# Graph attention on one core: rows gathered in plain edge order, each step a pair of an aligned group of 512 edges and a node tile

## The reference, cut to what matters

```
h = (x @ W).reshape(n, heads, ch)
e = alpha_src[src] + alpha_dst[dst];  e = where(e > 0, e, 0.2 * e)
m = segment_max(e, dst);  ex = exp(e - m[dst]);  s = segment_sum(ex, dst)
msg = h[src] * (ex / (s[dst] + 1e-16))[:, :, None]
out = segment_sum(msg, dst) + b
```

## Time and profile before

| | us |
|---|---|
| median of 3 runs (8891.62 to 8900.51) | 8892.6 |
| span of the profiled execution, first to last instruction | 8886.9 |
| median less span (what lies around it) | 5.7 |

### The profile page before, as it was taken

One profiled execution on the slowest core, in us unless ns is written; L12 is line 12 of the kernel. 1 busy time (PEld: TensorE's weight loads), 2 busy tenths in 40 slices (PEclk: granted clock), 3 DMA queues, 4 the chain that ended last, 5 costly groups with the idle time before them and its releaser, 6 DMA issues.

```text
span 8886.9 us, 230055 instructions
## 1 busy us (share of the span) xinstructions
PE 6173.7 (69%) x49885; PEld 5210.5 (59%) x50563; DVE 6168.8 (69%) x25428; ACT 4847.6 (55%) x11854; POOL 6191.5 (70%) x7562
## 2 busy tenths in 40 slices
PE   2466666666599999984666666666646666666665
PEld 2365656556588888873555555545445555656564
DVE  7799833333267676757999999999856666666665
ACT  4133333333245555534777777777647777777775
POOL 0377777777777777735777777777647777777775
PEclk9988888888899999986888888888755555555555
DMA  4233222222232323312222222222421111111114
GB/s 141 52 63 63 62 63 62 63 62 62 61 90 85 86 85 86 85 35 56 55 55 55 55 55 55 56 55 56 47 25 29 29 29 29 29 29 29 29 29 28
DMA packets 990923, 493.64 MB, mean 56 GB/s; under 512 B 830674, under 2 KB 841604, under 8 KB 990276
## 3 DMA queue, kind: packets, MB, share of 16 engines
q0 software_dynamic: 168832, 302.29, 15.6%
q1 hardware_dynamic: 701892, 169.48, 10.2%
q10 hardware_dynamic: 119840, 18.68, 1.3%
HBM read 356.53 MB, written 151.48 MB: 57 GB/s over the span
## 4 chain that ended last, share of the span: by engine, by line
issue 26%; POOL 21%; PE 20%; DVE 15%; DMA 7%; ACT 7%; DVEq 3%; ACTq 1%; POOLq 0%; SPq 0%; another core or an unknown queue 0%
POOL z_s L639 13%; POOL arena L689 8%; DMA arena<-table,arena 6%; PE ps_all L961 5%; PE ps_all L971 5%; ACT arena L825 3%; PE ps_all L984 3%; PE ps_all L981 2%; DVE arena L1494 2%; PE ps_all L1069 1%; ACT arena L857 1%; DVE arena L1580 1%; PE ps_all L993 1%; DVEq L385 1%; DVE ps_all L1232 1%
## 5 line engine op out<-in xcount | busy, mean ns | idle before, releaser
L689 POOL DMA_INDIRECT arena<-table,arena x3616 | 3527.3, 975 | 1421.4 <-issue 963.9
L639 POOL DMA_INDIRECT z_s<-arena x1660 | 1591.9, 959 | 850.8 <-issue 479.6
L1093 PE MATMUL ps_all<-arena 128*128 128x132 f32 (+1 forms) x7232 | 1584.7, 388 | 1.8 <-DVE acc L1597 1.8
L1093 PEld LDWEIGHTS ps_all<-arena 128*128 128x128 f32 x7232 | 1405.9, 288 | 2.7 <-issue 2.6
L1069 PE MATMUL ps_all<-ident_b,arena 128*128 128x128 bf16 x3616 | 465.3, 270 | 1311.8 <-DMA arena<-table,arena 1191.7
L825 ACT ACTIVATE arena<-lanes_b,arena 128x128 bf16<-128x128 bf16 x3616 | 1144.9, 386 | 349.1 <-DVE arena L1467 342.2
L1069 PEld LDWEIGHTS ps_all<-ident_b,arena 128*128 128x128 bf16 x3616 | 282.3, 117 | 1478.6 <-issue 844.4
L1494 DVE TENSOR_REDUCE arena<-ps_all 128x2 f32<-128x1024 f32 x904 | 1098.5, 1215 | 39.0 <-PE ps_all L1110 37.6
L849 ACT ACTIVATE arena<-ps_all 28x512 bf16<-28x512 bf16 (+1 forms) x904 | 527.5, 584 | 956.8 <-PE ps_all L1069 955.8
L744 ACT ACTIVATE arena<-ps_all 18x512 f32<-18x512 f32 x415 | 243.3, 586 | 1211.9 <-PE ps_all L948 1180.1
L1110 PE MATMUL ps_all<-arena,pick 128*128 128x512 bf16 x1809 | 694.6, 489 | 54.6 <-DVE arena L1494 24.3
(11 more groups left out here) (259 smaller groups left out, 15032.7 us busy)
## 6 DMA issues: line engine op xcount, KB each, us to landing
arena<-z_s SPq DMA_DIRECT2D x452, 264.0 KB, 2.7
arena<-table,arena POOLq DMA_INDIRECT x3616
arena<-rec_d SPq DMA_DIRECT2D x1660, 10.0 KB
z_s<-arena POOLq DMA_INDIRECT x1660
rec_d<-in_rec ACTq DMA_DIRECT2D x1, 16160.0 KB, 59.0
arena<-ids_d SPq DMA_DIRECT2D x904, 4.0 KB
arena<-pos_d SPq DMA_DIRECT2D x830, 0.5 KB
arena<-pos_d ACTq DMA_DIRECT2D x830, 0.5 KB
```

The costliest lines, as they stand in the source:

```text
L639: pool.indirect_dma_start(z_s, bass.IndirectOffsetOnAxis(ap=slot[:, g.slot(SLOTS), u:u + 1], axis=0), z_out[:, g.slot(SLOTS), u, :], None) ...
L689: pool.indirect_dma_start(g_rows[:, r, u * step + CODE_WORDS:(u + 1) * step], None, tables[n], bass.IndirectOffsetOnAxis(ap=ids[:, r, 0, u ...
L1093: mm = pe.matmul(ps[6][:, 0:out_w], a_hot_f[:, g.slot(4), u, :], g_msg[:, g.slot(4), u * out_w:(u + 1) * out_w], start=(u == 0), stop=(u = ...
```

## The change

The rows are no longer gathered group by group of the tiles, but in plain edge order: QUADS = 403 aligned groups of 512 edges cover all edges. One step ("visit") takes one pair of such an aligned group and a node tile that has edges in it. An aligned group that a tile boundary crosses is visited twice, so there are VISITS = 403 + 49 - 1 = 451 steps.

- SP and POOL run over the 403 aligned groups (`quad_pipeline`, peel 16, body 16); PE, ACT and DVE run over the 451 visits, with peel 16 and body 8 as before.
- `g_rows` becomes a ring of 16 aligned groups. SP loads only source numbers, and for group q waits for the messages of the last visit of group q - 16, read from a new table `done_by`.
- POOL waits for the landing of the previous aligned group before the last of its four gathers, and then counts it in `quads_in`.
- DVE finds the aligned group of a visit by register arithmetic (`quad_of`: visit number less tile number), and from it the ring slot for `logits` and `messages`, and the place of the destination numbers. These lie in SBUF for the whole layer (`node_of`), brought once by a DMA of 51,584 runs of 16 bytes that ACT issues at the start of the edge MLP.
- The codes no longer stand beside the gathered row but in a tile of their own (`coded`). A new DVE operation, `share_parts`, copies the three bf16 parts from the ring into it, after waiting for `quads_in`; PE transposes `coded` (32 columns) once that copy is done.

```diff
+QUADS = LINEAR // GE
+VISITS = QUADS + NT - 1
+RING = 16
+def quad_pipeline(eng, step, layer, each_round=None):
+    pipelined(eng, QUADS, 0, step, layer * QUADS, peel=RING, unroll=RING, each_round=each_round)
...
-                        sp.wait_ge(S("a_lane_ready"), g.back(SLOTS).done())
+                        sp.wait_ge(S(f"quads_in{n}"), Group(g.i, g.off - SLOTS, 0).done())
                         sp.sem_inc(S("sp_go"), 1)
-                        sp.wait_ge(S("neg_lane_ready"), g.back(SLOTS).done())
+                    if g.back(RING).exists():
+                        sp.wait_ge(S("msg_ready"), (freed.of(g.back(RING)) & COUNT_MASK) + n * VISITS)
...
-                    if g.back(SLOTS).exists():
-                        pool.wait_ge(S("msg_ready"), g.back(SLOTS).done())
-                        pool.wait_ge(S("turned"), g.back(SLOTS).done())
...
                     for u in range(U):
+                        if u == U - 1 and g.back(1).exists():
+                            landed(g.back(1))
...
+                def landed(g):
+                    pool.wait_ge(S(f"gathered_{g.slot(LANDING)}"), g.uses(LANDING, 16 * U))
+                    pool.sem_inc(S(f"quads_in{n}"), 1)
...
+            act.dma_start(node_of.rearrange("p (q u) -> p q u", u=U), ids_d[1:2, 0:LINEAR].rearrange("a (q p u) -> p (a q) u", p=P, u=U)
+                          ).then_inc(S("nodes_in"), 16)
...
-                        pe.wait_ge(S(f"gathered_{r}"), g.uses(SLOTS, 16 * U))
+                        pe.wait_ge(S("parts_ready"), g.done())
...
+                def quad_of(g):
+                    return (g.at - buckets.of(g)).with_bounds(min_val=0, max_val=QUADS - 1)
+                def gathered_rows(g):
+                    at = ((quad_of(g) & (RING - 1)) * slot_words).with_bounds(min_val=0, max_val=(RING - 1) * slot_words)
+                    return g_rows[:, bass.ds(at, U * row)]
...
-                    dve.tensor_tensor(lane, node, first, ALU.subtract).then_inc(S("a_lane_ready"), 2)
-                    dve.tensor_tensor(minus, first, node, ALU.subtract).then_inc(S("neg_lane_ready"), 2)
+                    for k, v in enumerate(visits):
+                        dve.tensor_tensor(lane[:, k, :], node_of[:, bass.ds(quad_of(v) * U, U)],
+                                          first_node[:, bass.ds(v.at, 1)].broadcast_to([P, U]), ALU.subtract).then_inc(S("a_lane_ready"), 1)
+                    dve.tensor_scalar(minus, lane, -1.0, None, ALU.mult).then_inc(S("neg_lane_ready"), m)
...
+                def share_parts(g):
+                    if g.back(SLOTS).exists():
+                        dve.wait_ge(S("turned"), g.back(SLOTS).done())
+                    parts = gathered_rows(g).bitcast(BF16).rearrange("p (u w) -> p u w", u=U)
+                    dve.wait_ge(S(f"quads_in{n}"), (quad_of(g) & COUNT_MASK) + 1)
+                    dve.sem_inc(S("dve_go"), 1)
+                    dve.tensor_copy(coded[:, r, :, CODE:CODE + 3 * heads], parts[:, :, 0:3 * heads]).then_inc(S("parts_ready"), 1)
...
                     for part in (shifts, codes, shifts):
                         next(part, None)
+                    share_parts(of(0))
```

More of the change, by code:

```diff
@@ L150, in attention_pipeline @@
 def attention_pipeline(eng, depth, step, layer, each_round=None):
-    pipelined(eng, GROUPS, depth, step, layer * GROUPS, peel=2 * SLOTS, unroll=SLOTS, each_round=each_round)
+    pipelined(eng, VISITS, depth, step, layer * VISITS, peel=2 * SLOTS, unroll=SLOTS, each_round=each_round)
+def quad_pipeline(eng, step, layer, each_round=None):
+    pipelined(eng, QUADS, 0, step, layer * QUADS, peel=RING, unroll=RING, each_round=each_round)
 class Chain:
@@ L240, in gnn_kernel @@
         group_tables = sb("group_tables", [64, ROW_GROUPS], I32)
-        bucket_of, first_edge = group_tables[0:1, :], group_tables[32:33, :]
+        bucket_of, done_by = group_tables[0:1, :], group_tables[32:33, :]
         src_tables = sb("src_tables", [64, ROW_GROUPS], I32)
@@ L263, in gnn_kernel @@
         tile_end = sb("tile_end", [NB, 3])
-        gap_wide = [sb(f"gap_wide{k}", [NB, P]) for k in range(2)]
+        tile_quad = sb("tile_quad", [NB, 1])
+        gap_wide = sb("gap_wide", [NB, P])
         here_lane = sb("here_lane", [P, 2])
@@ L673, in _ @@
                 pool.wait_ge(S("table_out"), 16 * (n + 1))
-                step = CODE_WORDS + row
                 def gather_rows(of):
@@ L1455, in edge_codes @@
                         return
+                    visits = [g] if h is None else [g, h]
+                    last, m = visits[-1], len(visits)
                     r, q = g.slot(SLOTS), g.slot(4)
-                    codes = g_rows[:, r:r + 2, 0:U * step].bitcast(BF16).rearrange("p k (u w) -> p k u w", u=U)
-                    lane, minus = lane_int[:, q:q + 2], neg_lane[:, q:q + 2]
-                    bits = lane_bits[:, q:q + 2]
-                    node = ids[:, r:r + 2, 1, :]
-                    first = first_node[:, bass.ds(g.at, 2)].unsqueeze(2).broadcast_to([P, 2, U])
@@ L1462, in edge_codes @@
-                    for k in (g, h):
-                        dve.wait_ge(S(f"ids_in_{k.slot(SLOTS)}"), k.uses(SLOTS, 16))
-                    dve.tensor_tensor(lane, node, first, ALU.subtract).then_inc(S("a_lane_ready"), 2)
-                    if h.back(4).exists():
-                        dve.wait_ge(S("a_hot_ready"), h.back(4).done())
-                    dve.tensor_tensor(minus, first, node, ALU.subtract).then_inc(S("neg_lane_ready"), 2)
+                    codes = coded[:, r:r + m]
+                    lane, minus = lane_int[:, q:q + m], neg_lane[:, q:q + m]
@@ L1554, in logits @@
                     r = g.slot(4)
-                    rows = g_rows[:, g.slot(SLOTS), 0:U * step].rearrange("p (u w) -> p u w", u=U)[:, :, CODE_WORDS:]
+                    rows = gathered_rows(g).rearrange("p (u w) -> p u w", u=U)
                     found = ps[5][:, 0:U * 2 * heads].rearrange("p (u w) -> p u w", u=U)
@@ L1600, in attend @@
                 def attend(of):
-                    ahead = of(-1)
-                    codes = edge_codes(of(0), ahead) if ahead is not None and ahead.off % 2 == 1 else iter(())
+                    now, ahead = of(0), of(-1)
+                    codes = edge_codes(now, ahead) if now is not None and now.off % 2 == 0 else iter(())
                     large, shifts = largest_shares(of(3)), new_shifts(of(4))
```

114 lines of the change are left out of this document (64 added, 50 removed).

## The result

The changed kernel takes 9521.4 us (median of 4 runs, 9515.7 to 9527.7) beside 8895.8 for the kernel before (4 runs, 8891.6 to 8900.5): ratio 1.0705, 95% interval 1.0692 to 1.0718. The forecast of a slower kernel was right, the 9255 us were not: the time lies 266 us above them and 11 above the end of the range.

The account below looks back on a forecast made before the run. It took POOL's gather pace to bound both attention layers, with DVE close behind in layer 1. Layer 1 +428, layer 2 -126 and edge MLP +64 gave +366 us, say 9255 us, range 9000 to 9500.

Parts of the forecast that it names:

- layer 1's mechanism: Attention layer 1: DVE's added work and turn lengthen a round from 41.5 to 49.0 us; with the ends, +428 us.
- layer 2's gain: Attention layer 2: a round falls from 40.5 to 38.1 us, -130 us; with the ends, -126 us.
- the base: DVE's own pace before the change: 40.6 us a round in layer 1, 32.1 in layer 2.
- Gather pace: POOL's gathers, fewer after the change, would need 37.1 us a round in layer 1 and 36.1 in layer 2.
- Additions to a DVE step: Added DVE operations and register work: 1.0 us a step, partly covered, taken as 0.7 in layer 1, 0.75 in layer 2.
- The turn: DVE's loop turn in layer 1: the larger body brings instruction fetches as in layer 2, +2.8 us a round.
- Rival B: Layer 1's enlarged DVE loop still turns without fetches: 151 us less than forecast, 9105 us; chance 0.18.
- Table loads: DVE's peel and end steps outside the loops: 98 added loads of 0.65 us, 55 us a layer taken as seen.
- Edge MLP: Start of the edge MLP: ACT's DMA of 51,584 short runs delays SP's first loads, 64 us taken, 0 to 100 possible.
- A: Rival on DVE's steps: sequencer additions hide entirely, only 0.13 us of engine time a step is added; 8660 us, chance 0.15.
- C: Rival on DVE's steps: nothing shared between uses, 1.2 us or more a step, with a second stall; 9650 us, chance 0.07.
- D: Rival on share_parts: DVE's new wait ties it to the gather, layer 2's -126 becomes about +270; 9650 us, chance 0.05.

Follow-up runs that it names:

- exp_early: Changed kernel with ScalarE's exponential issued ahead of the Relu instead of behind it: 9398.9 us, 1.0562 of the kernel before.
- three_gathers: Kernel before with three gathers a group in place of four, output not the reference's: 8370.7 us, 0.9408 of the kernel before.
- before_seq8_again: Kernel before with eight additions to an unused semaphore at the end of each DVE step: 9310.4 us, 1.0465 of the kernel before.
- before_shift_again: Kernel before with 60 unused semaphore additions on DVE ahead of layer 1, moving its loops: 9025.3 us, 1.0145; in a slower set 12221.5 us, 0.999.
- once_only_again: Changed kernel with each table entry loaded once per engine outside the loops, not once per use: 9436.2 us, 1.0603 of the kernel before.
- align: Changed kernel with 190 unused semaphore additions on DVE ahead of layer 1, moving its loops: 11893 us, 0.971 of 12235; run again 9516.1 us.
- before_three: Same kernel as three_gathers (kernel before, three gathers a group), run in a slower set: 10357.6 us, 0.847 of 12235.

## Why the prediction was wrong, step by step

The direction and layer 1's mechanism were right. The step that failed is layer 2's "32.1 + 8 x 0.75 = 38.1 us a round, above POOL's 36.1, against 40.5 now: -2.4 x 54 = -130". The round came out at 41.37, and layer 2's gain became a loss. What the sum lacks is a wait: DVE's message product stands waiting for ScalarE's exponential, an engine that the step did not look at. With that wait taken away (exp_early) the round is 39.01, so it is worth 2.36 of the 3.27 us that the round was off. The rest is small: the base measured 32.29 (three_gathers), and what is left over both, (39.01 - 32.29) / 8 = 0.84 us a step, stands for the additions, where 0.75 were taken. This split has an open end. The measured base holds 1.0 us of the same wait; if that is taken off it, the additions are 0.97 us a step (an estimate) and the wait's growth only some 1.3 us. No run separates the two.

- **Gather pace.** Right as a floor: 36.1 us a round in layer 2 was reached when everything else was out of the way (36.08, 35.98, 36.02). In the changed kernel it never bound.
- **Additions to a DVE step.** 0.7 us taken in layer 1, measured (50.76 - 44.27) / 8 = 0.81, both with fetches at the turn. The body grew by 79 instructions a round (340 to 419), 9.9 a step. At before_seq8_again's 0.078 us each they make 0.77 us, and the copy 0.1 more. The 0.1 us that the forecast took for one is near the 0.095 at which they follow one another. The cover was mis-sized: 0.3 of 1.0 us a step was taken off, and before_seq8_again shows 0.13 of 0.76. In layer 2 the body grew by 82.
- **The turn.** The fetches came to layer 1 as forecast (the gap in after is 4.30 where it was 1.27). Their price was taken as 2.8 us on DVE's own pace and measured 3.26 there. Layer 1's round is thus 50.76 in place of 49.0: 0.4 for the base (41.01, not 40.6), 0.5 for the turn, 0.9 for the additions. Rival B fails for the changed kernel: place decides for a body of 340 instructions, as before_shift_again shows, but none of the places tried made one of 419 fit. The page that I named there, the Trainium skill's Runtime: NRT & Kernel Launch (section "Instruction fetch mechanics"), has blocks of 256 instructions, two held. These traces differ, and decide: DVE's fetches of 8192 bytes come some 128 instructions apart, and a body of 373 that lies in 374 instructions from a boundary already fetches.
- **Table loads.** 55 us a layer taken for 98 loads. The trace has 93 more a layer, and once_only_again prices one at 0.5 us, which makes some 47: near, a little high.
- **What the sum left out.** It gave the additions to 54 rounds, that is 432 of 451 steps; the other 19 cost some 16 us a layer (an estimate, 19 x 0.84). The fill ahead of the first product grew by 20 and 12 us. Together layer 1's ends came 24 us, layer 2's 31 us above the forecast.
- **Edge MLP.** +64 taken, nothing found: PE is busy 1465.5 of the 1492 us, and SP's first load of the stage is issued at 2455.55, at 2454.27 before. The step that failed is the time of the transfer: ACT issues it at 2417.88, 38 us ahead of SP's first load and not a few, and it has landed 32.1 us later, before that load:

```profile
L781 ACTq DMA_DIRECT2D arena<-ids_d x1: 408/408/408, 2417.9 to 2417.9; - x1
...
DMA to landing us min/median/max: 32.1/32.1/32.1
```

  The two never met. So this trace does not show whether ACT's short runs would hold SP's issues up, nor can it bear out or contradict the Trainium skill's page that I named (DMA: Bandwidth & Descriptors, section "Issuing engines are not separate DMA queues"), by which they interleave.

The account of the miss, in us of the span: layer 1's rounds (9.33 in place of 7.5) x 54 = +99; layer 2's (+0.9 in place of -2.4) x 54 = +178, of which the wait is 2.36 x 54 = 127; ends and fills +55; MLP -64. Sum +268; the span is 270 above the forecast's 8886.9 + 366. That the total came within 3% owes something to luck: the MLP's 64 us, which did not come, hid a fifth of the miss.

Of the rivals, A fails by seq8: the sequencer's work hides only by a sixth. C's 1.2 us a step was too much (0.81), and there was no second stall. D fails: L1523 hardly waits (3.8 us in 1000, all "issue"). Why ScalarE's squares come so late in after was not tested; the timeline shows only that they wait for DVE's L1498.

## What to carry to other kernels

Price register and semaphore instructions by their count in the built loop, 0.08 us each on DVE here, wherever an engine's stream sets the pace, and take little cover for them. When a step on one engine gets later, follow each engine that waits for it and what stands in its queue ahead of the answer: the wait that took most of layer 2's gain back was for one instruction behind two others on ScalarE. And count the loop body against the blocks of fetched code: here that was worth 150 to 240 us in a layer (2.84 to 4.4 us a round), about as much as the faster gather pace in layer 2 (4.4 us a round).

## What the runs showed of the hardware

- **Fetches.** By the instruction counts of the built loops and the places of their fetches, a DVE loop turned without fetches only when it lay inside three blocks of 128 instructions and ended at least 12 short of the third boundary: 340, 335, 363 and 361 instructions, and 371 ending 12 short; with fetches 340 and 335 at other places, 371 at another place, 373 ending 10 short, and 399 to 419 wherever they lay. The gap at such a turn was 3.9 to 5.5 us, without fetches 1.1 to 1.5.
- **The first packet of a gather.** Where POOL had stood idle for over 4 us, it follows the gather's start by 1.65 us (118 such gathers in after, median).
- **The same program 35 to 38% slower.** In three of eight sets of runs the kernel before took 12017 to 12236 us; the record has chips 12 and 13 in sets of either kind. The first packet of a gather is no later there (1.66 us in before_shift, counted in the same way). DVE stands in waits of up to 9 us whose releaser the trace does not show (before_shift, 5500 to 6500):

```profile
DVE arena L1562 <- remote: 243.2, 41, 9.0
```

  The edge MLP takes its usual time there (SP's loads for it span 1407 us in before and in before_shift), edge ordering and attention do not. The order of the kernels turns: after with align is 2.9% faster than before, where align_again is 7.0% slower, and before_three is 15.3% faster, where three_gathers is 5.9%. Both issue fewer gathers than before; that this is why they gain there is a guess. What causes this condition is open.
